# Step 0 rewritten, and in every later step the output projection moved ahead of the quantised layer, with two PSUM banks alternating by step

## The reference

```python
# x (16, 512, 512), ctx (16, 120, 384), 16 heads of 32
h = layernorm(x)
q, k, v = h @ Wq + bq, ctx @ Wk + bk, ctx @ Wv + bv      # split in heads
o = softmax(q k^T / sqrt(32)) v                          # merged heads
x = x + tanh(g_xattn) * (o @ Wo + bo)
h = layernorm(x)
s = max(max|h| over a row, 1e-6) / 127
z = clip(round(h / s), -128, 127)                        # int8
x = x + tanh(g_ffn) * ((z @ weight_q^T) * s * weight_scale + bias)
```

## Time and profile before

| | |
|---|---|
| runs (3) | 800.2 us median, 796.23 to 801.88 |
| profiled execution | 797.8 us, span 796.0 us |
| granted TensorE clock | 0.999 |
| busy share PE, ACT, DVE, POOL | 96%, 76%, 68%, 65% |
| DMA | 177.24 MB, mean 223 GB/s |

### The profile page before, as it was taken

How to read it: one execution, slowest core, us unless ns; L and a number is a source line. 1 busy time by engine, 2 the same in 40 slices (tenths; PEclk the granted TensorE clock), 3 DMA queues, 4 the chain that set the end, 5 groups by cost and what they waited for, 6 DMA issues and landing times.

```text
span 796.0 us, 16271 instructions
## 1 busy us (share of the span) xinstructions
PE 767.5 (96%) x5883; PEld 529.6 (67%) x5938; DVE 543.6 (68%) x863; ACT 607.5 (76%) x846; POOL 520.7 (65%) x546
## 2 busy tenths in 40 slices
PE   9998989999999999999999999999999999999996
PEld 6665566676676676667667676667667667666563
DVE  5967767575686667667676667757568665755568
ACT  5766858787786877968687786778779687787785
POOL 4428465594856758575694957759485675855588
PEclk9999999999999999999999999999999999999999
DMA  8667798878698697869778788787879867666722
GB/s 291 232 196 201 225 288 229 236 228 255 193 283 230 197 271 223 241 199 312 216 194 272 211 266 217 229 258 227 254 195 284 216 183 227 199 174 178 207 64 106
DMA packets 115199, 177.24 MB, mean 223 GB/s; under 512 B 35888, under 2 KB 45488, under 8 KB 113072
## 3 DMA queue, kind: packets, MB, share of 16 engines
q1 hardware_dynamic: 88336, 128.14, 52.4%
q10 hardware_dynamic: 26784, 48.06, 22.7%
HBM read 120.03 MB, written 56.13 MB: 221 GB/s over the span
## 4 chain that ended last, share of the span: by engine, by line
PE 83%; issue 4%; DVE 4%; DMA 3%; ACT 2%; POOL 2%; SPq 1%; ACTq 0%; DVEq 0%; POOLq 0%
PE bank_b L432 28%; PE bank_a L432 18%; PE scores L487 8%; PE sum_ps L538 7%; PE scores L530 6%; PE pv_ps L542 6%; PE bank_a L586 4%; PE bank_b L586 2%; PE bank_a L561 1%; PE scores L432 1%; DMA k_rows<-k_parts 1%; SPq L235 1%; DVE row_max L1288 1%; PE sum_ps L502 1%; DMA wk_stage<-in_wk 1%
## 5 line engine op out<-in xcount | busy, mean ns | idle before, releaser
L1288 DVE TENSOR_REDUCE row_max<-scores 128x16 f32<-128x1920 f32 x64 | 137.9, 2154 | 15.4 <-PE scores L487 15.2
L1662 POOL TENSOR_TENSOR o_lo<-on,o_hi 128x512 fp32r<-128x512 f32 x48 | 62.8, 1309 | 112.2 <-ACT o_hi L962 112.2
L942 ACT ACTIVATE probs<-scores 120x2048 f32<-120x2048 f32 x64 | 120.1, 1877 | 20.5 <-PE scores L530 20.4
L1317 DVE SCALAR_TENSOR_TENSOR q_parts<-bank_b,bq_c,q_parts 128x512 fp32r<-128x512 f32 x45 | 33.8, 750 | 135.7 <-ACT q_parts L895 135.7
L487 PEld LDWEIGHTS scores<-k_sb,q_sb 32*128 32x128 f32 x1952 | 60.0, 186 | 54.2 <-issue 41.5
L1670 POOL TENSOR_TENSOR x<-x,gbias_r 128x512 f32<-128x512 f32 x64 | 83.0, 1298 | 17.4 <-ACT cen L968 16.3
L1656 POOL TENSOR_TENSOR x<-x,gbo_r 128x512 f32<-128x512 f32 x64 | 82.0, 1292 | 5.1 <-DMA x<-in_x 5.0
L1620 POOL TENSOR_TENSOR xt<-xt,rstd_b 128x512 f32<-128x512 f32 x56 | 85.3, 1561 | 0.0
L1675 POOL TENSOR_TENSOR x<-x,u_sb 128x512 f32<-128x512 f32 x56 | 72.6, 1296 | 6.8 <-DVE u_sb L1393 6.6
L432 PE MATMUL bank_b<-xt_hi,wq_hi 128*128 128x512 f32 x188 | 75.2, 400 | 0.0
L487 PE MATMUL scores<-k_sb,q_sb 32*128 32x120 f32 x1952 | 71.2, 282 | 3.3 <-ACT q_sb L873 2.3
(11 more groups left out here) (246 smaller groups left out, 1947.2 us busy)
## 6 DMA issues: line engine op xcount, KB each, us to landing
q_stack<-q_rows ACTq DMA_DIRECT2D x180, 256.0 KB, 4.5
q_rows<-q_parts SPq DMA_DIRECT2D x60, 512.0 KB, 5.6
xt<-in_x_t SPq DMA_DIRECT2D x16, 1024.0 KB, 8.2
x<-in_x SPq DMA_DIRECT2D x64, 256.0 KB, 4.6
out_x<-x SPq DMA_DIRECT2D x61, 256.0 KB, 3.1
x_in<-in_x SPq DMA_DIRECT2D x60, 256.0 KB, 5.4
k_stack<-k_rows SPq DMA_DIRECT2D x90, 120.0 KB, 4.8
k_rows<-k_parts SPq DMA_DIRECT2D x30, 240.0 KB, 3.2
```

The source lines that it names most:

```text
L942: act.activation(probs[0:KEYS], scores[0:KEYS], ACT.Exp, scale=SCALE).then_inc(p_ready, 1)
L1288: dve.tensor_reduce(row_max[:].rearrange("p (t r) j -> p r t j", r=ROWG)[:, :, :, j], scores[:, :, 0:QT * KEYS].rearrange("p r (t k) -> p ...
L1662: pool.tensor_tensor(o_lo[i % 2][j], on[:], o_hi[i % 2][j].bitcast(F32), ALU.subtract).then_inc(o_split, 1)
```

## The change

Four things. (1) TensorE, ScalarE, VectorE and POOL get a first_step in place of step(0): each query projection of batch 1 but the first is issued behind the scores by query of the slot before, and the splits and stores of pair 1's keys all move into step 1. SP's order up to step 2 follows. (2) In every slot the output projection stands directly behind the scores by query (in slot 0 behind the keys or values), and the quantised layer last, in slot 3 behind turn_max. (3) banks_of(i) swaps the two banks by the parity of the step. (4) The waits follow: query projections 1 to 3 of a step wait for the residual of the quarter before; VectorE does residual and statistics before dequantise; POOL does add_out(m, 0) behind low_o(i, 3). The last step is unchanged but for one wait.

The core of the diff, with its indent cut by eight. In TensorE's and VectorE's step the removed lines are left out; they stand in the code above.

```diff
+def banks_of(i):
+    return (bank_b, bank_a) if i % 2 == 1 else (bank_a, bank_b)
...
     store_k(0, 1)
     stack_k(1, 0)
     load_x(2, 2)
+    store_q(1, 0)
     load_x(2, 3)
-    store_q(1, 0)
-    store_k(0, 2)
     load_x(3, 0)
+    store_q(1, 1)
     load_x(3, 1)
     store_rstd(2)
+    store_k(0, 2)
     load_rstd(2)
-    store_q(1, 1)
-    store_k(0, 3)
     load_x(3, 2)
     load_x(3, 3)
+    store_q(1, 2)
+    store_k(0, 3)
+    load_x(4, 0)
     stack_k(1, 1)
-    store_q(1, 2)
-    store_k(1, 0)
-    load_x(4, 0)
     store_rstd(3)
     store_q(1, 3)
-    store_k(1, 1)
+    load_x(4, 1)
+    load_ctx(2)
+    load_rstd(3)
     load_residual(0, 0)
     load_residual(0, 1)
     load_residual(0, 2)
-    load_x(4, 1)
     load_residual(0, 3)
-    load_ctx(2)
-    load_rstd(3)
     load_xt(3)

...
+        if i == 1:
+            store_k(1, 0)
...
-        if is_batch(k_of(i)):
+        if i == 1:
+            store_k(1, 1)
+        elif is_batch(k_of(i)):
...
+        if i == 1:
+            stack_k(2, 0)

         if is_batch(k_of(i)):
-            store_k(k_of(i) // 2, 2 * (i % 2) + 1)
+            store_k(k_of(i) // 2, 2 * (i % 2) + (i > 1))
...
+        if i == 1:
+            store_k(1, 3)
+            stack_k(2, 1)
...
+    def first_step():
+        pe.wait_ge(max_done, nth(0, DT, 3))
+        scores_by_key0(0)
+        pe.wait_ge(v_ready, nth(1, 1))
+        project_q(1, 0, bank_b)
+        attend(0, 0)
+        scores_by_query(1, 0)
+        project_q(1, 1, bank_a)
+
+        pe.wait_ge(max_done, nth(1, DT, 0))
+        scores_by_key0(1)
+        pe.wait_ge(q_split, nth(0, DT, 0))
+        project_k(1, 0, bank_b)
+        project_k(1, 1, bank_b)
+        attend(0, 1)
+        scores_by_query(1, 1)
+        pe.wait_ge(k_ready, nth(1, DT, 1))
+        project_q(1, 2, bank_b)
+
+        pe.wait_ge(max_done, nth(1, DT, 1))
+        scores_by_key0(2)
+        pe.wait_ge(q_split, nth(0, DT, 1))
+        project_v(2, bank_a)
+        attend(0, 2)
+        scores_by_query(1, 2)
+        pe.wait_ge(v_ready, nth(2, 1))
+        project_q(1, 3, bank_a)
+
+        pe.wait_ge(max_done, nth(1, DT, 2))
+        scores_by_key0(3)
+        pe.wait_ge(q_split, nth(0, DT, 2))
+        project_k(1, 2, bank_b)
+        project_k(1, 3, bank_b)
+        attend(0, 3)
+        scores_by_query(1, 3)
+        pe.wait_ge(q_split, nth(0, DT, 3))
+        fold_bias(bank_a, range(DT - 1))
+        pe.wait_ge(log_done, nth(0, DT, 3))
+        turn_max(1, sum_ps)
+        fold_bias(bank_a, range(DT - 1, DT))
+
     def step(i):
         e, m, b, n = i - 2, i - 1, i + 1, i + 2
         keys_next = is_batch(n) and n % 2 == 0
         values_next = is_batch(n) and n % 2 == 1
         pair = n // 2
+        one, two = banks_of(i)

         pe.wait_ge(max_done, nth(i, DT, 3))
         scores_by_key(i, 0)
         if i == 1:
+            pe.wait_ge(k_ready, nth(1, DT, 3))
+        else:
+            pe.wait_ge(u_ready, nth(e, QT, 0))
+        project_q(b, 0, one)
         pe.wait_ge(v_ready, nth(i, 1))
         attend(i, 0)
         scores_by_query(b, 0)
+        pe.wait_ge(q_split, nth(b - 1, DT, 0))
+        if keys_next:
+            project_k(pair, 0, one)
+            project_k(pair, 1, one)
+        if values_next and i > 1:
+            project_v(n - 1, one)
+        if i == 1:
+            pe.wait_ge(bias_folded, 1)
+        elif b % 2 == 0:
             pe.wait_ge(k_ready, nth(b // 2, DT, 3))
+        else:
             pe.wait_ge(v_ready, nth(b, 1))
+        pe.wait_ge(o_split, nth(m, DT, 3))
+        project_o(m, 0, two)
         if keys_next:
             pe.wait_ge(k_ready, nth(pair, DT, 1))
         if values_next:
             pe.wait_ge(v_ready, nth(n - 1, 1))
         if is_batch(e):
+            quantised_layer(e, 1, one)
+
+        pe.wait_ge(max_done, nth(b, DT, 0))
+        scores_by_key(i, 1)
+        pe.wait_ge(x1_ready, nth(m, QT, 0))
+        project_q(b, 1, two)
+        if is_batch(e):
             pe.wait_ge(u_ready, nth(e, QT, 1))
+            turn_z(e, 1, one)
         attend(i, 1)
         scores_by_query(b, 1)
+        if is_batch(e):
+            pe.wait_ge(zt_ready, nth(e, 2, 1))
+        project_o(m, 1, one)
+        pe.wait_ge(q_split, nth(b - 1, DT, 1))
+        if is_batch(e):
+            quantised_layer(e, 2, two)

         pe.wait_ge(max_done, nth(b, DT, 1))
         scores_by_key(i, 2)
+        pe.wait_ge(x1_ready, nth(m, QT, 1))
+        project_q(b, 2, one)
         attend(i, 2)
         scores_by_query(b, 2)
+        if is_batch(e):
+            pe.wait_ge(u_ready, nth(e, QT, 2))
+        project_o(m, 2, two)
         pe.wait_ge(q_split, nth(b - 1, DT, 2))
+        if is_batch(e):
+            quantised_layer(e, 3, one)

         pe.wait_ge(max_done, nth(b, DT, 2))
         scores_by_key(i, 3)
+        pe.wait_ge(x1_ready, nth(m, QT, 2))
+        project_q(b, 3, two)
         if is_batch(e):
             pe.wait_ge(u_ready, nth(e, QT, 3))
+        turn_z(m, 0, one)
         attend(i, 3)
         scores_by_query(b, 3)
+        pe.wait_ge(zt_ready, nth(m, 2, 0))
+        project_o(m, 3, one)
         pe.wait_ge(log_done, nth(i, DT, 3))
         turn_max(b, sum_ps)
+        pe.wait_ge(q_split, nth(b - 1, DT, 3))
+        if i == 1:
+            pe.wait_ge(rows_ready, 1)
+        quantised_layer(m, 0, two)
+        pe.wait_ge(x1_ready, nth(m, QT, 3))
         if i == LAST - 1:
+            quantised_layer(m, 1, one)
+        if keys_next:
+            project_k(pair, 2, one)
+            project_k(pair, 3, one)
         if values_next:
+            project_v(n, one)

...
+        exponentials(0, 1)
+        bias_q(1, 1, bank_a)
+        split_high(1, 1)
+        bias_k(1, 0, bank_b)
+        bias_k(1, 1, bank_b)
+        log_sums(0, 1)
+        invert_sums(0, 1)
+        split_high0(3)
+        split_high_k(0, 2)
+        high_o(0, 1)
+
+        exponentials(0, 2)
+        bias_q(1, 2, bank_b)
+        split_high(1, 2)
+        stack_q(1, 0)
+        copy_v(2, bank_a)
+        log_sums(0, 2)
+        invert_sums(0, 2)
+        split_high_k(0, 3)
+        high_o(0, 2)
+
+        exponentials(0, 3)
+        bias_q(1, 3, bank_a)
+        split_high(1, 3)
+        stack_q(1, 1)
+        bias_k(1, 2, bank_b)
+        bias_k(1, 3, bank_b)
+        high_x(2, 0)
...
+        if i == 1:
+            split_high_k(1, 0)
...
+        if i == 1:
+            split_high_k(1, 2)
...
+        if i == 1:
+            split_high_k(1, 3)
...
+        scale_q1(1, bank_a)
+        x_statistics(2, 1)
+        x_statistics(2, 2)
+        split_low(1, 1, bank_a)
+        x_statistics(2, 3)
+        maxima(1, 1)
+        normalise_o(0, 1)
+
...
+        split_low(b, 0, one)
         if is_batch(e):
             quant_max(e, 2)
             quant_max(e, 3)
             quant_factors(e, 1)
+        maxima(b, 0)
         normalise_o(i, 0)
+        residual(m, 0, two)
+        x1_statistics(m, 0)
+        if is_batch(e):
+            dequantise(e, 1, one)
+
+        if is_batch(f):
             x_statistics(f, 1)
+        split_low(b, 1, two)
+        maxima(b, 1)
         normalise_o(i, 1)
+        residual(m, 1, one)
+        x1_statistics(m, 1)
+        if is_batch(e):
+            dequantise(e, 2, two)
+
+        if is_batch(f):
             x_statistics(f, 2)
+        quant_max(m, 0)
+        quant_max(m, 1)
+        quant_factors(m, 0)
+        split_low(b, 2, one)
+        maxima(b, 2)
         normalise_o(i, 2)
+        residual(m, 2, two)
+        x1_statistics(m, 2)
+        if is_batch(e):
+            dequantise(e, 3, one)

         if is_batch(f):
             x_statistics(f, 3)
+        split_low(b, 3, two)
+        maxima(b, 3)
+        low_max(b)
+        residual(m, 3, one)
         normalise_o(i, 3)
         if is_batch(n):
             low_x(n, 0)
+        dequantise(m, 0, two)
         if is_batch(n):
             low_x(n, 1)
             low_x(n, 2)
             low_x(n, 3)
+        x1_statistics(m, 3)
         if i == LAST - 1:
+            dequantise(m, 1, one)

...
-        if is_batch(m) and i < LAST - 1:
-            add_out(m, 0)
+        if i == 1:
+            low_k(1, 2)
         low_o(i, 3)
-        if i == 0:
-            low_k(1, 1)
-        if i == LAST - 1:
-            add_out(m, 0)
-        if i == 0:
-            pool.wait_ge(bias_folded, 1)
-            bias_x(i, 0)
-            bias_x(i, 1)
+        add_out(m, 0)
+        if i == 1:
+            low_k(1, 3)
```

More of the change, by code:

```diff
@@ L828, in _ @@
             pe.wait_ge(wk_lo_done, CT)
-            step(0)
+            first_step()
             pe.wait_ge(wo_lo_done, 2)
@@ L1035, in step @@
                 if keys_next:
-                    bias_k(pair, 0, bank_b)
-                    bias_k(pair, 1, bank_b)
+                    bias_k(pair, 0, one)
+                    bias_k(pair, 1, one)
                 if values_next and i > 1:
-                    copy_v(n - 1, bank_b)
+                    copy_v(n - 1, one)
                 high_o(i, 0)
@@ L1080, in step @@
```

(39 more changed lines are left out.)

274 lines of the change are left out of this document (78 added, 196 removed).

## The result

The changed kernel takes 808.8 us (median of 4 runs, 808.65 to 808.92), the kernel before 798.2 in the same comparison (4 runs, 795.88 to 801.88): ratio 1.013, 95% interval 1.010 to 1.017. The profiled execution took 808.91 us, span 807.1, granted clock 0.998. The forecast was 801.5 within 794 to 810, with "within 1%" as the likeliest class. The time is inside the range and 7.3 us above the forecast, and the class is the next one: slower by a little over 1%. The kernel before took 800.4, 799.8 and 798.1 us in the later sessions; against these the loss would be 8.4 to 10.7 us.

The account below looks back on a forecast made before the run. Steady steps were taken as bound by TensorE's issue rate. Terms -4.6 + 5.3 + 1.4 - 0.3 = +1.8 us on the profiled 797.8 gave 799.6; the median of runs was forecast at 801.5, range 794 to 810.

Parts of the forecast that it names:

- Part 1: Steps 0 and 1: earlier query projections remove TensorE's waits, less 1.5 us of new waits; -4.6 us.
- The bound of +5: Steps 0 and 1: upper bound, in us, if a key store of pair 1 again lands after 11.14 us.
- Part 2: Steady slots: new order exposes a longer weight load, 0.10 us in each of 53 slots; +5.3 us.
- part 3a: Slot 0 of even steps: quantised layer waits for bias_k's copy out of its bank, 0.24 us in 6 steps; +1.4 us.
- the -0.3 of the last step: Start of the last step: low_o comes a little earlier, cutting 0.3 us from the 1.4 us wait.
- 3b: Slots 1 to 3: query projections wait for the previous residual, covered, tightest in slot 2 by 0.3 us; cost nothing.
- Parts 3b to 3d: Steady slots: residual waits, slot 0's query split wanted earlier, and POOL's add_out 4 us later; each costs nothing.
- residuals too late: Rival, slots 1 to 3: query projections wait for residuals, 0.4 us in 39 slots, 15.6 us, 815; chance 0.12.
- one slot of each step: Cheaper form of the late-residual rival: only one slot per step waits, 5 us, 807; no separate chance.
- The 53 gaps are real: Rival: the 0.16 us idle ahead of each quantised layer is a real cost, giving back 8.4 us, 788; chance 0.06.
- The loads cost alike: Rival: bf16 and fp32r weight loads take equal time, so the new slot order costs nothing, 796; chance 0.10.
- The start doesn't gain: Rival, steps 0 and 1: a pair 1 key store lands late, start gives 0 to +3, 806 to 809; chance 0.12.

Follow-up runs that it names:

- e1: Changed kernel, with POOL's bias_x1 made to wait until VectorE's low_max is done: 807.8 us, ratio 1.013.
- e4: Kernel before, with only the new first_step, SP's new queue order and pair 1's key splits in step 1: 793.5 us, ratio 0.994.
- e6: Changed kernel, with POOL's bias_x1 waiting for low_max and ScalarE's key/value copies ahead of the roundings of the layer's input: 802.6 us, ratio 1.003.
- e7: Changed kernel, with turn_max behind slot 3's quantised layer and ScalarE's key/value copies ahead of the roundings of the layer's input: 798.7 us, ratio 0.997.
- e3: Changed kernel, with the quantised layer ahead of the output projection again in slots 1 and 2: 840.0 us, ratio 1.052.
- e5: Changed kernel, with ScalarE's slot 0 copies of keys or values ahead of the two roundings of the layer's input: 806.4 us, ratio 1.010.
- e2: Changed kernel, with turn_max behind the quantised layer in slot 3 instead of ahead of it: 807.3 us, ratio 1.009.
- e8: e7 with the last split of pair 1's keys, its store and stacking moved from step 1's end into step 2's slot 0: 799.7 us, ratio 1.002.

## Why the prediction was wrong by 7 us

Against the profiled execution the miss is larger: the sum gave +1.8 us on 797.8, and 808.9 was measured, 9.3 more than 799.6. The forecast had put 1.9 on top for the median of the runs. That 808.8 lies inside the range is luck: its upper end came from a start without gain or a late slot 2, and neither occurred.

**Part 1 (start), -4.6: the sign and the mechanism right, the term too small.** Measured -6.7 from the first scores of step 0 to those of step 2, a little past the bound of -6.5; the waits of the earlier trace rows are gone, all of them. The 1.5 us that I had set aside for new waits did not come, except 0.3 us on the maxima and 0.3 on q_stack: in the stretch from 38.6 to 122.9 the list of the changed kernel has just these two. The bound of +5 was not idle: in e1, e4 and e6 ScalarE waited for a key store behind the reordered splits, and step 2 took 52.0 to 52.9 us instead of some 48 (47.2 in e4), in e1 and e4 with part of it at the lower clock. In the changed kernel's own profile it cost nothing.

**Part 2 (order), +5.3: right.** Slots 1 and 2 are longer by 0.10 and 0.09. e7, in which almost no wait is left in the steady steps, takes 573.3 us for steps 2 to 13, 6.1 more than before. 48 slots at 0.10 are 4.8. Its even steps from 4 on are longer by 0.38 to 0.42, four slots at 0.10; the odd ones by about 0.5 and steps 2 and 11 by 0.8 and 0.9, and that is the rest. Where that rest comes from is not shown. That the order makes the tenth is shown: it is gone in e4 and, from scores by query to scores by key, in slot 1 of e3. That it is an exposed weight load I still only argue: behind the scores by query the first output matmul takes 0.33 us to the next, all others 0.23 to 0.24 (191.45, 191.78, 192.02).

```profile
191.45 0.50 PE L443 MATMUL bank_b<-wo_hi,o_hi 128*128 128x512 f32 x1
191.78 0.40 PE L443 MATMUL bank_b<-wo_lo,o_hi 128*128 128x512 f32 x1
192.02 0.40 PE L443 MATMUL bank_b<-wo_hi,o_lo 128*128 128x512 f32 x1
```

**The step that failed: "because turn_max now comes 0.8 us earlier".** The prediction used that as a gain for ScalarE (part 3a, and the -0.3 of the last step, which did not come: the wait for o_lo_end is 1.4 us as before) and never asked for what turn_max waits. The layer had been its cover, like the covers of the query projections in 3b, which I did count. The list of waits of before had no row for it, which is why I passed it over; a cover is not in that list, only its lack is. Worth: 8.0 us in 13 waits, 0.6 each, which is more than the whole difference between forecast and result. Two things made it up. The order took 0.8 us of cover, which left the chain of the maxima none. Then low_max itself went from 0.22 to 0.72 us, because VectorE no longer had dequantise in front of it and it fell under an operation of POOL. e1 shows that this second part decides: with low_max at 0.23 the waits are 0.8 us in all, and turn_max is 0.09 late in most steps.

The rows say what kind of contention it is: low_max ends 0.09 us behind POOL's operation and takes 0.22 when that is kept away; its 0.91 us are the 0.82 until POOL is done (215.63 to 216.45) and little more. The Trainium skill, "SBUF — State Buffer", section "SBUF: two separate sides", says that VectorE and GpSimd share a port pair as an exclusive lock, held for the whole instruction, which a VectorE operation with two SBUF inputs also needs against a GpSimd one that reads SBUF. The trace agrees with it here: low_max has both inputs in SBUF, as bias_x1 has, and in all twelve of steps 2 to 13 it ends 0.07 to 0.09 us behind bias_x1. By that rule the price of such an overlap is what is left of POOL's instruction, by estimate up to the 1.3 us that these take (the longest low_max took 1.10), however small VectorE's own is.

**Part 3a (copies of the keys), +1.4, bounds 0 to 3: right in kind, low in size.** The prediction had the copies 0.44 us late and 0.2 back. Measured: up to 0.5 late, 2.2 us in 5 waits, and 0.8 for the values of the odd steps, which I had not looked at. e5 gives the price of both: 3.0 us. But a term's bounds hold only with the others fixed: once the stall in slot 3 was taken away (e1), the same wait was 4.0 us, it seems because ScalarE had lost those 0.6 us too; e6, which moves the copies, has none.

**Parts 3b to 3d, nothing: right.** No residual is waited for; the split of the query in slot 0 and add_out show nowhere. The *residuals too late* rival, the one for the slower side, had the right form (a cover of a TensorE group gone, VectorE's chain behind it, once per step) at the wrong place. Its cheaper form, "one slot of each step", had been priced at 5 us and 807; the place that came true cost 9.4. (The rivals' times do not all start alike: 815 is 15.6 on the 799.6 of the sum, 807 and 788 start from 801.5.)

**The rivals on the faster side.** *The 53 gaps are real*: refuted, the rows are gone and the slots are longer. *The loads cost alike*: refuted by slots 1 and 2 at +0.10. *The start doesn't gain*: refuted for the changed kernel.

**The sum as it should have been**, to the start of step 15's scores: start -6.7, the later begin of step 0 +0.6 (39.19 against 38.62; the other profiles have 38.8 to 40.1, so this is none of the change's), order +4.8, copies +3.0, and turn_max with what it drags along +9.5, together +11.2 (measured 751.74 - 740.51 = 11.2). The last term is a remainder: steps 2 to 13 grew by 17.3, less 4.8 and 3.0. Twelve times the 0.78 us by which turn_max starts late are 9.4. Of it 7.7 us are the waits in the list; the other 0.14 a step is not in the list, which counts from the modelled end of the last output matmul (215.68 + 0.39 = 216.07) and not from 215.91.

## What to carry to other kernels

When a group is moved from ahead of B to behind it, B loses a cover: list everything that B waits for, with the time at which that is ready, even where the list of waits has no row for it. A row of zero there says nothing of the room that is left. Once one stall on a full engine is mended, look at the next queue before the time is read: two late helpers in series (here VectorE's low_max and ScalarE's copies) must be mended together, and each alone looks like little gain (1.5 and 2.4 us alone, 10.1 together). Price a wait of TensorE by the clock behind it as well as by its length. And of a change with several parts, measure the parts: here the start alone is the fastest kernel (793.5), and the new order of the slots, even with its waits mended, costs 6.1 us in steps 2 to 13 and gives nothing there. By the runs alone e4 and e7 are not clearly apart (ratios 0.994 [0.989, 0.998] and 0.997 [0.993, 1.001]).

## What the runs showed of the hardware

- A small VectorE operation on SBUF (128x64, two inputs, 0.22 us) takes 0.72 us in the mean and 0.91 in the case shown when an operation of GpSimd runs over it (it ends 0.07 to 0.09 us behind that one, so it costs what is left of it), and 0.23 once GpSimd waits for it.
- Issuing three q_stack transfers holds ScalarE's queue for 1.8 us (224.80 in the changed kernel), and the next operation (inv_sum) is 1.33 us late for it, on an engine that is busy 75% of the time. The late copy of the keys stands four operations further down; whether it would be in time without the issue, no run tries.

```profile
224.80 1.79 ACTq L859 DMA_DIRECT2D q_stack<-q_rows  x3
226.69 0.60 ACT L967 ACTIVATE inv_sum<-sum_ps 128x512 f32<-128x512 f32 x1 [1.33 <-issue]
```

- The wait of ScalarE for one 240 KB key store at the end of step 1 varies between executions of nearly the same queues: none in the changed kernel's profile and in e7's, 1.0 us in e4's, 2.9 in e6's.
- TensorE's granted clock falls behind some of its idle stretches and not behind others of the same length. Behind 2.49 us idle it was 0.53 for the next 1.7 us in e1 (0.50 is the lower level, 1.2 GHz), behind 2.47 us in e6 it stayed at 1.00. Behind the 1.36 us wait for o_lo_end in the last step it was 0.50 in e2 and in e8 (for 3.3 us in each), and 1.00 in the changed kernel. Where it fell, it stayed down for 3 to 6 us and cost 1.4 to 2.7 us on top of the wait. Why it falls in one execution and not in the other, the traces do not say. How much of the spread of the runs it makes, the single profiles cannot say.
